# Where the first expert tiles' row gathers and index copies stand in the queues at the end of cross attention

## The chip, the core and the metric

One NeuronCore of a Trainium2 chip runs the whole kernel. The metric is the device time of one execution in microseconds (us); lower is better. The engines are TensorE (PE in the profile; its weight loads are PEld), VectorE (DVE), ScalarE (ACT), GpSimd (POOL) and SyncE (SP), which here only issues DMAs. Each engine works through its own queue in order, and they wait for one another on semaphores.

## The reference

A decoder block in fp32 on x of shape (4, 1024, 256), with post-norm after each of three parts:

```python
x = layernorm(x + gated_delta_attention(x))      # 4 heads, causal conv, recurrent state
x = layernorm(x + cross_attention(x, ctx, len))  # 16 heads of 64 over 77 context rows
x = layernorm(x + moe_ffn(x))                    # 8 experts, the best 2 of each token

# cross attention, for each token and head
scores = q @ k.T / 8 ; scores[:, col >= len] = -1e9
o = softmax(scores) @ v ; y = o @ Wo
# experts
probs = softmax(x @ router_w.T) ; keep the top 2, renormalised
h = silu(x @ gate_w[e] + gate_b[e]) * (x @ up_w[e] + up_b[e])
y = sum over the two e of probs[e] * (h @ down_w[e] + down_b[e])
```

## The kernel before, in words

The 4096 tokens are 32 tiles of 128 (`TILES`), in 8 blocks of 4 (`BLOCKS`, `BLK`). Four stages run one after the other: `project_stage`, `delta_stage`, `cross_stage`, `final_stage`. The experts are part of `cross_stage`: each engine's queue there is written out by hand, first its part of cross attention, tile by tile (`g` = 4n + t for tile t of block n), then its part of the experts' 71 tiles of 128 gathered rows (`FT`), numbered j.

Cross attention of tile g goes: scores in PSUM (TensorE, L1906), scaled out to `sc` (VectorE, L2278), mask added (GpSimd, `add_mask`, L1814), maximum taken and subtracted (VectorE, L2286, L2288), exponential (ScalarE, L2053), sum and reciprocal `den` (VectorE, `sums`, L2294, L2296), multiplied by `den` (GpSimd, `normed`, L1820). Then TensorE turns the weights (`weights_turned`, L1921, 10 transposes in three groups), ScalarE takes each group out of PSUM (L2062, L2065, L2067), and TensorE multiplies with the values (`attended`, L1930). The scores of tile g come two tiles ahead of its weights, so tile 31, the last, has no scores behind it to fill TensorE's queue. VectorE adds the residual for each pair of tiles (L2306).

While attention runs, the router works on blocks that are done: logits (TensorE, L1954), softmax and top two (VectorE, `shifted_logits`, `top_two`), positions of each row in its expert's list (`entries`, with the additions to `cum` at L2190), and the entries written to a `list` in HBM by indirect DMAs from GpSimd (`listed_rows`, L1805). In the last block, at t = 2 (tile 30), TensorE computes the logits of block 6 behind the attention of tile 30 and VectorE copies them out (`logits_out`, L2152). After five blocks the list holds enough full tiles for the first 32 expert tiles (`HEAD`), which can therefore start before the routing is complete.

An expert tile j needs: its 128 list rows (`expert_sync`, SP, L2461, to `rows`), their token numbers as integers (`expert_indices`, VectorE, L2611, to `idx`), an indirect gather of the tokens' rows of x2 from HBM (`expert_gather`, GpSimd, L2478), two transposes (TensorE, `x_turned`, L2522) taken out by ScalarE (L2581), gate and up products (L2533), the biases added by VectorE (L2624), SiLU by ScalarE (L2586), the product (VectorE, L2630), its transposes (L2543), the down product (L2554), bias and weight (L2637, L2639), and an indirect scatter with addition (GpSimd, L2492). Rows are loaded `LIST_LEAD` = 3 tiles ahead and gathered `ROW_LEAD` = 2 tiles ahead, so `rows` and `idx` of tiles 0, 1 and 2 and the gathers of 0 and 1 are issued during the last tiles of cross attention.

SP loads the down weights and bias (`load_experts_late`) and the gate and up biases (`load_experts_last`, L2419, two loads of 2 MB) in the last block. VectorE waits for them ahead of its first expert tile; the bias tile lies where attention's queries of odd blocks did.

The one wait of a gather that matters here, in `expert_gather`: `pool.wait_ge(x.idx_done, j + 1)`. `expert_indices` waits for `rows_in`.

Of the kernel before, what the change touches and what calls it, by code (L numbers as in the profile page):

```python
# [1631 lines left out]
def cross_stage(nc, a, s):  # L1632

    with ExitStack() as ctx:
# [77 lines left out]
        x = Experts(s, sem, x2_out, list_out, listed, at_done, row_bytes, row_idx,  # L1712
                    xs=[cut(of_kT, 0, D), cut(of_kT, D, D), cut(of_kT, 2 * D, D), cut(of_aT[1], 0, D)],
                    xsT=[cut(of_kT, 3 * D, D), cut(of_aT[1], D, D)],
                    g=[cut(sc[0], q * FF, FF) for q in R], u=[cut(sc[1], q * FF, FF) for q in R],
                    hT=[cut(of_aT[0], q * FK * P, FK * P) for q in R], o=[cut(of_vw, q * D, D) for q in range(4)],
                    pG=S[0:2], pU=[S[2], TB[0]], pX=TB[1], pH=Q, pD=O)
# [7 lines left out]
        TILE_N = BLOCKS * BLK  # L1725
# [56 lines left out]
        @block.gpsimd  # L1782
        def _(pool):
            nc.gpsimd.memset(powers[:], -0.5).then_inc(set_up, 1)
            nc.gpsimd.memset(eps[:, 1:2], XD * EPS).then_inc(set_up, 1)

            nc.gpsimd.memset(ent[:], 0.0).then_inc(set_up, 1)
            nc.gpsimd.memset(ids[:], 0.0).then_inc(set_up, 1)
            pool.wait_ge(set_up, 4)
            for t in T:  # L1790
                for k in R:
                    nc.gpsimd.tensor_scalar(ids[:, t, k, 1:2], con[:, C_COL:C_COL + 1],
                                            float(t * P), None, ALU.add).then_inc(set_up, 1)
                nc.gpsimd.tensor_scalar(ids[:, t, :, 2], con[:, C_COL:C_COL + 1].broadcast_to([P, 2]), float(t * P), None,
                                        ALU.add).then_inc(set_up, 1)
            for e in range(NE):
                nc.gpsimd.memset(cum[:, BLK, e:e + 1], float(e * REGION * P)).then_inc(set_up, 1)
            nc.gpsimd.tensor_scalar(k128[:], con[:, C_IOTA:C_IOTA + TILES], float(P), None, ALU.mult).then_inc(set_up, 1)

            def listed_rows(m, tiles):  # L1800

                pool.wait_ge(placed, m + 1)
                for t in tiles:
                    for k in R:
                        nc.gpsimd.indirect_dma_start(  # L1805
                            out=s["list"], out_offset=bass.IndirectOffsetOnAxis(ap=idx[:, k, t:t + 1], axis=0),
                            in_=ent[:, t, k, :], in_offset=None).then_inc(list_out, 16)

            def add_mask(g):
                b = g // BLK // 2  # L1810
                v = heads(sc[g % 2][:])
                pool.wait_ge(kv_in, 64 * b + 64)
                pool.wait_ge(sc_taken, 3 * g + 3)
                nc.gpsimd.tensor_tensor(v, v, madd[b % 2][:].unsqueeze(1).broadcast_to([P, XH, CTX]), ALU.add  # L1814
                                        ).then_inc(masked, 1)

            def normed(g):
                v = heads(sc[g % 2][:])
                pool.wait_ge(den_done, g + 1)
                nc.gpsimd.tensor_tensor(v, v, over_keys(den[g % 2][:]), ALU.mult).then_inc(scaled, 1)  # L1820

            def x2_deviations(n):
                pool.wait_ge(mv_done, n + 1)
                if n:
                    pool.wait_ge(x2_done, n)
                nc.gpsimd.tensor_scalar(rstd[:], mv[:, :, 1], EPS, None, ALU.add).then_inc(var_up, 1)
                pool.wait_ge(var_up, n + 1)
                nc.gpsimd.tensor_tensor(rstd[:], rstd[:], powers[:], ALU.pow).then_inc(r_done, 1)

            add_mask(0)  # L1830
            for n in range(BLOCKS):
                for t in T:
                    g = n * BLK + t
                    if g == TILE_N - 1:
                        for j in range(ROW_LEAD):
                            expert_gather(nc, pool, x, s, j)
                    normed(g)
                    if g + 1 < TILE_N:
                        add_mask(g + 1)
                    if n and t == 0:  # L1840
                        x2_deviations(n - 1)
                    if n >= 2 and t in (1, 2):
                        listed_rows(n - 2, (2 * t - 2, 2 * t - 1))

            def between(j):
                if j == 0:
                    x2_deviations(BLOCKS - 1)
                if 2 <= j < 2 + BLK:
                    listed_rows(BLOCKS - 2, (j - 2,))
                if 9 <= j < 9 + BLK:  # L1850
                    listed_rows(BLOCKS - 1, (j - 9,))

            expert_gpsimd(nc, pool, x, s, between)
            pool.wait_ge(list_out, 16 * BLOCKS * BLK * 2)
# [286 lines left out]
        def _(dve):  # L2141
# [115 lines left out]
            def rq_out(m):  # L2257
                dve.wait_ge(ssT_done, m + 1)
                if m:
                    dve.wait_ge(sc_taken, 3 * BLK * m)  # L2260
                sums = X[:].rearrange("p (t g i) -> p t g i", t=BLK, i=32)
                for k in range(2):
                    nc.vector.reciprocal(rq[:, :, 8 * k:8 * k + 8].rearrange("p t (g r) -> p t g r", r=2),
                                         sums[:, :, :, 2 * k:2 * k + 2]).then_inc((rq_half, rq_done)[k], 1)
# [65 lines left out]
            for n in range(BLOCKS):  # L2330
                for t in T:
                    g = n * BLK + t
                    if t == 2 and n + 1 < BLOCKS:
                        rq_out(n + 1)
                    if t == 2:
                        residual(n, 0)
                    if t == 0 and n:
                        residual(n - 1, 1)
                    if g + 1 < TILE_N:
                        maximum(g + 1)  # L2340
                        if t == 0 and n:
                            aggregated(n - 1)
                        sums(g + 1)
                    if t == 0 and n:
                        norm_terms(n - 1)
                    if g + 2 < TILE_N:
                        rider = None
                        if t == 2 and n:
                            rider = lambda frm, m=n - 1: logits_out(m, frm)
                        if t == 0 and n >= 2:  # L2350
                            rider = lambda frm, m=n - 2: counts_out(m, frm)
                        scaled_out(g + 2, rider)
                    if t == 2 and n == BLOCKS - 1:
                        dve.wait_ge(lg_done, 1)
                        logits_out(n - 1, X)
                    if t == 2 and n:
                        shifted_logits(n - 1)
                    if t == 3 and n:
                        top_two(n - 1)
                    if t == 0 and n >= 2:  # L2360
                        entries(n - 2)
                    if t and n == HEAD_BLOCKS + 1:
                        head_list(t - 1)
                    if g == TILE_N - 2:
                        for j in range(LIST_LEAD):
                            expert_indices(nc, dve, x, j)

            def between(j):
                if j == 0:
# [70 lines left out]
LIST_LEAD, ROW_LEAD = 3, 2  # L2440
# [24 lines left out]
def expert_gather(nc, pool, x, s, j):  # L2465

    q = j % 4
    if j == 0:
        pool.wait_ge(x.x2_out, 32 * HEAD_BLOCKS)
    if j == 3:  # L2470
        pool.wait_ge(x.at_done, BLOCKS * BLK)
    if j == HEAD:
        pool.wait_ge(x.x2_out, 32 * BLOCKS)
    pool.wait_ge(x.idx_done, j + 1)
    if j >= 4:
        pool.wait_ge(x.xT_done, j - 3)
    seen = HEAD_BLOCKS * BLK if j < HEAD else TILES
    nc.gpsimd.indirect_dma_start(  # L2478
        out=x.xs[q], out_offset=None, in_=s["x2"][0:seen].rearrange("t p d -> (t p) d"),
        in_offset=bass.IndirectOffsetOnAxis(ap=x.idx[j % 8][:, 1:2], axis=0)).then_inc(x.xs_in[q], 16)  # L2480
# [124 lines left out]
def expert_indices(nc, dve, x, j):  # L2605

    q = j % 8
    dve.wait_ge(x.rows_in[q], 16 * (j // 8) + 16)
    if j >= 8:
        dve.wait_ge(x.o_out[j % 4], 16 * (j // 4) - 16)  # L2610
    nc.vector.tensor_copy(x.idx[q][:], x.rows[q][:, 1:3]).then_inc(x.idx_done, 1)  # L2611
# [191 lines left out]
```

## Time and profile before

| | |
|---|---|
| median of 3 runs | 1705.97 us (1705.02 to 1707.05) |
| the profiled execution | 1707.56 us, its span 1705.8 us |
| mean granted TensorE clock | 0.951 |
| busy, share of the span | TensorE 89%, VectorE 64%, ScalarE 42%, GpSimd 39% |

Times in the trace count from the span's start. The change lies between 1190 and 1262 us; the expert tiles run from about 1237 to 1670, the final stage after that. A granted clock of 1.00 is TensorE's full speed (2.4 GHz), 0.50 half of it (1.2 GHz).

### The profile page before, as it was taken

The numbers are of one execution on the slowest core, as the hardware profiler recorded it, in microseconds if no ns is written. First come the engines' busy times: TensorE is split into PE (matmuls) and PEld (weight loads), VectorE is DVE, ScalarE is ACT, GpSimd is POOL, SyncE is SP. The second block draws the span as 40 slices with busy tenths as digits, with TensorE's granted clock in tenths as the row PEclk, the third lists the DMA queues.
The fourth block names the chain that finished last, engine by engine and source line by source line (L and its number), as shares of the span: only waits on it lengthen the run. The fifth ranks groups of instructions, "written<-read, shape, count | busy, mean of one in ns | idle before, by whom it ended". The sixth has DMA issues, their size and how long they took to land. (4 is left out here: it accounts for less than half of the span.)

```text
span 1705.8 us, 30447 instructions
## 1 busy us (share of the span) xinstructions
PE 1514.8 (89%) x10698; PEld 1075.5 (63%) x10698; DVE 1087.5 (64%) x2352; ACT 724.3 (42%) x1573; POOL 671.7 (39%) x526
## 2 busy tenths in 40 slices
PE   6999954799999999967999999997698999999990
PEld 3555523788888888643677777776555666666660
DVE  4899866577788875541458777888556444444543
ACT  4877751234444444454555455552242222222224
POOL 1354446212333311000434566654555544444440
PEclk9999976799999999989999999999799999999995
DMA  3233447645555535054034024110733332232226
GB/s 106 87 137 122 161 143 193 164 119 156 155 154 146 140 94 192 34 191 136 1 100 144 30 70 145 51 37 13 254 56 41 45 48 47 45 47 48 45 39 204
DMA packets 186795, 176.62 MB, mean 104 GB/s; under 512 B 79624, under 2 KB 147772, under 8 KB 186524
## 3 DMA queue, kind: packets, MB, share of 16 engines
q1 hardware_dynamic: 167659, 148.90, 28.8%
q0 software_dynamic: 17024, 22.43, 7.9%
q10 hardware_dynamic: 1968, 3.41, 0.7%
q8 instruction: 87, 1.43, 0.3%
q14 instruction: 57, 0.46, 0.1%
HBM read 110.67 MB, written 64.01 MB: 102 GB/s over the span
## 5 line engine op out<-in xcount | busy, mean ns | idle before, releaser
L2492 POOL DMA_INDIRECT y<-vw,idx x71 | 125.1, 1762 | 189.6 <-DVE vw L2639 178.3
L622 DVE SCALAR_TENSOR_TENSOR conv_y<-conv_in,taps,conv_y 128x512 f32<-128x512 f32 x192 | 161.4, 850 | 24.5 <-ACT conv_y L470 19.8
L2554 PE MATMUL xO<-late,aT 128*128 x568 | 134.5, 380 | 0.8 <-DVE vw L2637 0.8
L1876 PE MATMUL xQ<-late,last 128*128 128x512 f32 x256 | 124.8, 610 | 10.6 <-ACT late L2039 4.8
L2533 PE MATMUL xS<-w_gu,kT 128*128 x288 | 129.8, 593 | 0.4 <-issue 0.2
L375 PE MATMUL ps_j<-xnT,w_qkv 128*128 128x512 f32 x256 | 122.7, 603 | 0.0
L1820 POOL TENSOR_TENSOR sc<-sc,den 128x1232 f32<-128x1232 f32 x32 | 72.0, 2250 | 112.6 <-DVE den L2296 112.5
L2554 PEld LDWEIGHTS xO<-late,aT 128*128 128x128 f32 x568 | 102.4, 190 | 12.2 <-issue 1.2
L2624 DVE TENSOR_TENSOR sc<-xS,last 128x512 f32<-128x512 f32 x107 | 73.6, 691 | 54.3 <-PE xS L2533 50.6
L2637 DVE TENSOR_TENSOR vw<-xO,late 128x256 f32<-128x256 f32 x71 | 30.1, 424 | 119.5 <-PE xO L2554 110.0
L1814 POOL TENSOR_TENSOR sc<-sc,madd 128x1232 f32<-128x1232 f32 x32 | 82.7, 2585 | 32.7 <-DVE sc L2278 32.7
L2533 PEld LDWEIGHTS xS<-w_gu,kT 128*128 128x128 f32 x288 | 54.5, 190 | 54.1 <-issue 52.4
L1805 POOL DMA_INDIRECT list<-ent,idx x64 | 74.6, 1166 | 35.0 <-DVE ent L2204 18.2
L1000 POOL DMA_DIRECT2D x<-x1t x28 | 16.0, 572 | 183.4 <-ACT x1t L1352 183.4
L1930 PE MATMUL xO<-vw,aT 128*128 128x256 f32 (+1 forms) x320 | 78.8, 405 | 4.0 <-DVE x2t L2306 2.9
L1876 PEld LDWEIGHTS xQ<-late,last 128*128 128x128 f32 x256 | 45.2, 192 | 52.6 <-issue 31.2
L2294 DVE TENSOR_REDUCE den<-sc 128x16 f32<-128x1232 f32 x32 | 45.9, 1436 | 49.0 <-ACT sc L2053 49.0
L2581 ACT ACTIVATE kT<-xT 128x256 f32<-128x256 f32 x36 | 13.8, 382 | 146.8 <-PE xT L2522 142.5
L2581 ACT ACTIVATE aT<-xT 128x256 f32<-128x256 f32 x35 | 13.4, 383 | 146.2 <-PE xT L2522 141.8
L1930 PEld LDWEIGHTS xO<-vw,aT 128*128 128x128 f32 (+1 forms) x320 | 64.7, 205 | 16.7 <-issue 5.4
L1930 PE MATMUL xO<-last,aT 128*128 128x256 f32 (+1 forms) x320 | 72.0, 380 | 0.0
L1921 PE MATMUL xT<-con,sc 128*128 128x128 f32 x320 | 48.8, 287 | 25.8 <-POOL sc L1820 25.3
(359 smaller groups left out, 3664.2 us busy)
## 6 DMA issues: line engine op xcount, KB each, us to landing
carried<-qkvg SPq DMA_DIRECT2D x64, 256.0 KB, 4.0
qkvg<-tok SPq DMA_DIRECT2D x4, 2048.0 KB
qkvg<-gate SPq DMA_DIRECT2D x8, 1024.0 KB
qks<-qkvg SPq DMA_DIRECT2D x32, 256.0 KB, 4.6
steps<-step SPq DMA_DIRECT2D x30, 256.0 KB, 4.4
qkvg<-carried SPq DMA_DIRECT2D x3, 2048.0 KB
vw<-even SPq DMA_DIRECT2D x4, 1232.0 KB
xin<-in_x SPq DMA_DIRECT2D x9, 512.0 KB, 10.0
```

What stands on the lines that cost most here:

```text
L375: mm = pe.matmul(ps_j[j % 2][:], w_qkv[:, c, j * P:(j + 1) * P], xnT[b][:, c, :], start=c == 0, stop=c == KD - 1)
L622: y = nc.vector.scalar_tensor_tensor(conv_y[m % 4][:], conv_in[b][:, m, k:k + BT], taps[:, m, k:k + 1], conv_y[m % 4][:], ALU.mult, ALU.add)
L1805: nc.gpsimd.indirect_dma_start(out=s["list"], out_offset=bass.IndirectOffsetOnAxis(ap=idx[:, k, t:t + 1], axis=0), in_=ent[:, t, k, :], in ...
L1814: nc.gpsimd.tensor_tensor(v, v, madd[b % 2][:].unsqueeze(1).broadcast_to([P, XH, CTX]), ALU.add).then_inc(masked, 1)
L1820: nc.gpsimd.tensor_tensor(v, v, over_keys(den[g % 2][:]), ALU.mult).then_inc(scaled, 1)
L1876: mm = pe.matmul(Q[:], w_q[:, c, j * P:(j + 1) * P], x1T[:, c, :], start=c == 0, stop=c == KD - 1)
L1921: mm = pe.transpose(TB[u % 2][0:rows(c), i * P:(i + 1) * P], sc[g % 2][:, c * P:c * P + rows(c)], ident)
L1930: mm = pe.matmul(O[:, (g % 2) * D:(g % 2 + 1) * D], aT[g % 2][0:rows(c), c, :], vw[b % 2][0:rows(c), c, :], start=c == 0, stop=c == KCH - 1)
L2492: nc.gpsimd.indirect_dma_start(out=s["y"].rearrange("t p d -> (t p) d"), out_offset=bass.IndirectOffsetOnAxis(ap=x.idx[j % 8][:, 0:1], axi ...
L2533: mm = pe.matmul(to[:], x.xsT[q][:, c, :], w_gu[:, bass.ds(e, 1), c, k * FF:(k + 1) * FF], start=c == 0, stop=c == KD - 1)
L2554: mm = pe.matmul(x.pD[:, 0:D], x.hT[q][:, k, :], w_d[:, bass.ds(e, 1), k, :], start=k == 0, stop=k == FK - 1)
L2624: nc.vector.tensor_tensor(to, frm[:], b_gu[:, bass.ds(e, 1), k * FF:(k + 1) * FF], ALU.add).then_inc(done, 1)
```

## The change

On GpSimd the two gathers of expert tiles 0 and 1, which stood ahead of the normalisation of tile 31, now stand behind it. On VectorE the three index copies (expert tiles 0 to 2), which were the last thing in the turn of tile 30, behind the router's logits of block 6, are now issued ahead of the wait for those logits, directly behind the sums of tile 31. No instruction is added or removed.

```diff
@@ gpsimd queue of cross_stage
                 for t in T:
                     g = n * BLK + t
+                    normed(g)
+                    if g + 1 < TILE_N:
+                        add_mask(g + 1)
                     if g == TILE_N - 1:
                         for j in range(ROW_LEAD):
                             expert_gather(nc, pool, x, s, j)
-                    normed(g)
-                    if g + 1 < TILE_N:
-                        add_mask(g + 1)
                     if n and t == 0:
                         x2_deviations(n - 1)
@@ vector queue of cross_stage
                     if t == 2 and n == BLOCKS - 1:
+                        for j in range(LIST_LEAD):
+                            expert_indices(nc, dve, x, j)
                         dve.wait_ge(lg_done, 1)
                         logits_out(n - 1, X)
...
                     if t and n == HEAD_BLOCKS + 1:
                         head_list(t - 1)
-                    if g == TILE_N - 2:
-                        for j in range(LIST_LEAD):
-                            expert_indices(nc, dve, x, j)
```

## Rows read from the trace of the kernel before

**Rows 1.** The page, part 2: TensorE's granted clock in 40 equal slices, in tenths.

```profile
PEclk9999976799999999989999999999799999999995
```

**Rows 2.** Busy time of each engine (instructions), clock, DMA share and GB/s by stretch.

```profile
1200.00:1220.00 20.00, 14.24 (x57) 11.49 (x55) 12.21 (x17) 4.50 (x7) 13.89 (x10) 0.74 0.92 315
1220.00:1240.00 20.00, 13.13 (x52) 9.86 (x52) 6.42 (x28) 2.06 (x6) 5.09 (x5) 0.74 0.49 173
1300.00:1320.00 20.00, 15.60 (x61) 9.47 (x60) 9.60 (x20) 5.13 (x10) 13.28 (x12) 1.00 0.31 35
1620.00:1640.00 20.00, 20.00 (x80) 12.78 (x79) 9.50 (x20) 5.63 (x12) 10.01 (x8) 1.00 0.33 46
```

**Rows 3.** Timeline, 1190 to 1262: start, length, engine, line, what, [idle before, releaser].

```profile
1197.50 3.01 SPq L2461 DMA_DIRECT2D rows<-list  x3
...
1199.19 4.19 PEld L1930 LDWEIGHTS xO<-vw,aT 128*128 128x128 f32 x20
...
1210.07 3.08 SPq L2419 DMA_DIRECT2D last<-in_L_ffn_up_b  x1
...
1217.20 0.25 DVE L2296 RECIPROCAL den<-den 128x16 f32<-128x16 f32 x1
...
1219.17 1.85 PE L1954 MATMUL xX<-w_r,x2T 128*128 128x8 f32 x16
...
1221.61 0.30 DVE L2611 CAST idx<-rows 128x2 int32<-128x2 f32 x3
1222.57 0.99 POOL L2478 DMA_INDIRECT kT<-x,idx  x1 [6.04 <-DVE idx L2611]
...
1224.86 2.25 POOL L1820 TENSOR_TENSOR sc<-sc,den 128x1232 f32<-128x1232 f32 x1
...
1227.17 2.49 PE L1921 MATMUL xT<-con,sc 128*128 128x128 f32 x10 [6.15 <-POOL sc L1820]
...
1230.18 6.36 PEld L1930 LDWEIGHTS xO<-vw,aT 128*128 128x128 f32 x20 [0.96 <-ACT aT L2067]
...
1236.57 0.36 PEld L2522 LDWEIGHTS xT<-con,kT 128*128 128x128 f32 x2
...
1239.86 0.69 DVE L2624 TENSOR_TENSOR sc<-xS,last 128x512 f32<-128x512 f32 x1 [0.92 <-PE xS L2533]
...
1242.09 1.28 ACT L2586 ACT_TABLE_LOAD   x1
...
1245.85 0.47 PEld L2543 LDWEIGHTS xQ<-con,sc 128*128 128x128 f32 x4
```

**Rows 4.** TensorE in short stretches: length, busy (instructions), clock, DMA share, GB/s.

```profile
1192.50:1195.00 2.50, 0.01 (x1) 1.00 0.00 0
1207.50:1208.00 0.50, 0.00 (x0) 0.50 1.10 372
1224.50:1225.00 0.50, 0.00 (x0) 0.50 1.07 410
```

**Rows 5.** Timeline, 1176 to 1184: transposes and last eviction of tile 28.

```profile
1177.95 0.86 PEld L1921 LDWEIGHTS xT<-con,sc 128*128 128x128 f32 x8 [3.10 <-POOL sc L1820]
...
1179.95 0.26 ACT L2067 ACTIVATE aT<-xT 80x128 f32<-80x128 f32 x1
```

**Rows 6.** DMA view, 1209 to 1245 (median us to landing); tile `rows`, 1190 to 1262.

```profile
last<-in_L_ffn_up_b SPq DMA_DIRECT2D x1, 2048.0 KB, 20.5
...
DMA to landing us min/median/max: 6.4/7.4/8.4
```

**Rows 7.** GpSimd's DMA queue, 1219 to 1226, then 1226 to 1229.5: packets, MB, share.

```profile
q0 software_dynamic: 36, 0.00, 0.4%
...
q0 software_dynamic: 96, 0.26, 18.7%
```

**Rows 8.** By line, ns min/median/max: L2190 whole run; L1805 from 1195 to 1225.

```profile
L2190 DVE TENSOR_TENSOR cum<-cum,cnt x32: 166/167/2512, 926.8 to 1289.0; 128x8 f32<-128x8 f32 x32
...
L1805 POOL DMA_INDIRECT list<-ent,idx x8: 954/984/2150, 1200.6 to 1215.6; - x8
```

## The prediction

> **What bounds the kernel now.** I began with the page's slices of TensorE's granted clock: full or nearly so but for a few slices, of which the one with a 7 in the second half (number 28 counted from 0) is 1194 to 1237 us [rows 1]. The kernel is one long chain on TensorE, so a microsecond of TensorE idleness is a microsecond of time unless something behind it gives it back. The table by stage places the hole: of the 40 us from 1200 to 1240 TensorE is busy for 27.4, at a mean clock of 0.74; in the expert tiles as at 1620 to 1640 it is busy for all of a 20 us stretch at full clock, with one exception, 15.6 of 20 us at 1300 to 1320 [rows 2]. The expert tiles are thus a block that should slide with its start.
>
> The timeline from 1190 shows how tile 31, the last of cross attention, is reached [rows 3]. VectorE has the reciprocal `den` at 1217.45. All that `normed(31)` needs is there, and GpSimd has been idle since 1216.53 (1222.57 less its 6.04 of idle time). But the two gathers stand ahead of `normed(31)`, and they need index copies that VectorE issues behind the router's logits, which TensorE ends at 1221.02. So the chain is: logits 1221.02, index copies 1221.61, first gather 1222.57, second behind it, `normed(31)` 1224.86 to 1227.11, transposes 1227.17. TensorE idles for 6.15 us, and the row names GpSimd's `sc` as the releaser.
>
> **The change, part by part.** (1) Index copies. They go from 1221.61 to the end of `sums(31)`, 1217.45. They must have their rows. SP issued the three row loads from 1197.50; the last issue ended at 1200.51, and row loads land 6.4 to 8.4 us after issue where the trace shows it, so the last is in by about 1209 [rows 3, 6]. Bound: the copies of before ran at 1221.61 and show no wait. I take none. What is queued behind them on VectorE is `logits_out`, which cannot start before 1221.02, so 3.6 us cover three copies of 0.3 us in all. Nothing else is moved on VectorE.
>
> (2) `normed(31)`. GpSimd is free and starts 0.1 us behind `den`: 1217.53 to 1219.8, at the 2.25 us of its row. The multiply is then no longer what ends TensorE's wait. TensorE itself is: it runs attention of tile 30 and the logits until 1221.02. Transposes start at 1221.0 instead of 1227.17. **Gain 6.15 us.**
>
> The copies now run beside `normed(31)`, both on SBUF. The trace hints at what that can do: of 32 tiny `cum` additions on VectorE the median took 167 ns and the longest 2512, about the length of one GpSimd pass over the scores; of the eight GpSimd list writes from 1200.6 on the median issue took 984 ns, the longest 2150 [rows 8]. The Trainium skill (SBUF — State Buffer, "Who interferes with whom") says that the two engines share a port pair as an exclusive lock, so that whoever comes second blocks for a whole instruction; it speaks against this placement, and these two maxima agree with it. By that rule the last copies wait for the multiply's end at 1219.8. The price, from the rows: the copies end at 1220.1 at the latest, the multiply at 1220.1 if the copies hold it up instead, and a gather's issue grows by up to 1.2 us. Logits end at 1221.02, so the first two cost nothing; the third falls on the gathers' margin below.
>
> (3) The clock. The clock goes by what TensorE did before. The weight loads of tile 29's attention ended at 1203.38, and the granted clock stood at half at 1207.5; TensorE stopped at 1221.02, and it stood at half at 1224.5; idle time from 1192.5 to 1195 left it at full [rows 3, 4]. With the hole gone it is still at full when tile 31's transposes start, and the longest pause after that is the ScalarE evictions, about 1 us. So I expect full clock throughout. Tile 31 at half clock took 3.01 us from first transpose to attention's first weight load (1227.17 to 1230.18); tile 28 at full took 1177.95 to the end of its last eviction at 1180.21, 2.25, with 0.05 on top 2.3 [rows 5]. **Gain 0.7.** Attention's weight loads took 6.39 us from 1230.18 to the turn of the first expert tile at 1236.57; tile 29's at full clock 4.19. **Gain 2.2.** The first expert turn would start at about 1227.5 instead of 1236.57.
>
> (4) The gathers. GpSimd issues them after the multiply, at 1219.9 and 1221.2, 2.7 us earlier than before, but they must now be in by 1227.5, where before they had until 1236.57. They share the DMA engines with the bias loads. Before, gather 0 was issued at 1222.57; up to 1226 its queue moved only small packets of the list writes (36, 0.00 MB), and then, between 1226 and 1229.5, the 96 packets of both gathers (0.26 MB) [rows 7]. So gather 0 lands between 3.4 and 6.9 us after issue: 1223.3 to 1226.8. I take 1225.8, nearer the late end since the DMA engines are full, in time by 1.7 us. Gather 1 is needed only at the second turn, 4.7 us after the first. The Trainium skill (DMA: Bandwidth & Descriptors, "Queues, rings and completion order") says that each DMA engine alternates between the queues that have work, so a gather is not behind the whole bias load; the trace agrees in that the gathers moved while the bias load, landed at 1230.6, was still under way.
>
> (5) The bias loads themselves. `up_b` was issued at 1210.07 and lands 20.5 us later, at 1230.6 [rows 6]. VectorE waits for it ahead of its first expert addition, at 1239.86 before, at 1230.8 in the new order: just not a wait. If it is one, there is room. The first tile's gate half waits for ScalarE's table load (1242.09 to 1243.37), and TensorE takes the product's transpose only at 1245.85 [rows 3]: from the first addition at 1239.86 that is 6.0 us for two additions, the activation and the product, which by their own lengths need about 4 (an estimate). So the landing may slip by some 1.5 us past 1230.8 and TensorE feels nothing. What VectorE has ahead of that wait is on time as well: it had sat idle for 0.92 us before 1239.86, thus was done at 1238.9, and all of that hangs on tile 31's evictions and attention and moves with them, to 1229.9.
>
> Sum: 6.15 + 0.7 + 2.2 = 9.05 us. The profiled execution took 1707.56 us around a span of 1705.8, so its like would take 1698.5. It lies 1.6 above the median of 1705.97; against the median the forecast is **1696.9 us**.
>
> **The rivals.** A, as above: 1696.9, own range 1696.0 to 1698.2 (the margins under (4) and (5) touched lightly, and the runs' spread of 1 us).
>
> B, a transfer takes the place of the wait: gather 0 or the bias load is late. For it speaks that the margins are 1.7 and about 1.5 us and the DMA engines are busy for 0.92 of 1200 to 1220 [rows 2]. At the worst gather 0 is in when the shared drain of before ended, 1229.5: the turn 2.0 us late, gain 7.0, 1698.9. Time 1697.8 to 1699.
>
> C, the clock falls anyway in tile 31 because of the pauses between its pieces: only the 6.15 us remain, 1699.8. Against it: full clock survived a longer pause at 1192.5 [rows 4].
>
> D, the gain is given back among the expert tiles, so that the time is within 0.2% of before. The place would be 1301 to 1318, where TensorE waits 4.4 of 20 us for gathers that stand behind GpSimd's scatters and list writes. Two such stretches more are 8.8 us and give 1705.7. Against it: these waits are between instructions that all slide together, and no load with a fixed date lies behind 1231.
>
> E, slower: the copies hold VectorE because the third tile's rows come late. What VectorE has to do from there to the first expert addition is its 6.42 us of work at 1220 to 1240 [rows 2]. That ends later than 1239.86 only if the rows come after 1233.4, and the kernel is 0.2% slower from 1236.8; the copies at 1221.61 exclude that for the execution traced. For an arrival at 1237.5 the time would be 4.1 above the median, 1710.1.
>
> The change not doing what it says: it would need TensorE to wait at 1221 for something else than `scaled`; but the row of 1227.17 names `sc` of GpSimd as what came last, so I give it nothing of its own.
>
> **How the numbers follow.** A 0.60, B 0.20, C 0.10, D 0.07, E 0.03. 0.2% is 3.4 us, about what a measurement of this kernel can tell from no change. A, B and C are all faster by more: 0.90, to which I add 0.02 of D that gives back only half; same 0.05, slower 0.03. The range takes in A, B and C with the runs' spread on both ends: 1695.3 to 1700.5.
>
> **What would show it.** Right: GpSimd's multiply L1820 for tile 31 starts 0.1 us after `den`, ahead of the gathers; TensorE's idle time before the last L1921 group is gone, the group takes less than 2.49 us, the clock is 1.0 from 1218 on; the first L2522 stands near 1227.5; everything from there to the end is 9 us earlier. Wrong: L2522 or the first L2624 waiting on a DMA (B), a half clock in attention 31 (C), more TensorE idle time than 5 us after the first 60 us of the expert tiles (D), copies L2611 long after `den` (E).

## The result

| | before | changed |
|---|---|---|
| median of 20 runs | 1706.96 us | 1698.7 us |
| lowest to highest | 1702.9 to 1714.33 | 1693.95 to 1706.1 |
| profiled execution, span | 1705.8 us | 1700.0 us |

The ratio is 0.9951 with a 95% interval of 0.9939 to 0.9963: 8.4 us faster, 6.3 to 10.4 at the interval's ends. The forecast was 9.05 us and 1696.9, from a median of 1705.97 over the first three runs; from the 1706.96 of all twenty it would be 1697.9. The ratios in this text leave out two runs at a granted clock of 0.55 and 0.64, one of e1_gathers_only (2663.37 us) and one of the kernel before beside e1 to e4 (2320.02 us).

The timeline of the changed kernel at the end of cross attention follows. Its columns are those of [rows 3], whose rows it answers to; from `expert` on, a line number is one lower than before (the gather is L2477, the first turn L2521, the bias addition L2623, the product's transposes L2542).

```profile
1213.67 2.70 SPq L2418 DMA_DIRECT2D last<-in_L_ffn_up_b  x1
...
1219.99 0.25 DVE L2296 RECIPROCAL den<-den 128x16 f32<-128x16 f32 x1
1220.16 0.24 DVE L2610 CAST idx<-rows 128x2 int32<-128x2 f32 x3
1220.33 2.24 POOL L1820 TENSOR_TENSOR sc<-sc,den 128x1232 f32<-128x1232 f32 x1 [1.01 <-DVE idx L2610]
...
1221.23 1.85 PE L1954 MATMUL xX<-w_r,x2T 128*128 128x8 f32 x16
1222.73 1.02 POOL L2477 DMA_INDIRECT kT<-x,idx  x1 [0.16 <-issue]
...
1222.94 1.07 PE L1921 MATMUL xT<-con,sc 128*128 128x128 f32 x8
...
1225.22 4.18 PEld L1930 LDWEIGHTS xO<-vw,aT 128*128 128x128 f32 x20 [0.79 <-ACT aT L2067]
...
1229.43 0.36 PEld L2521 LDWEIGHTS xT<-con,kT 128*128 128x128 f32 x2
...
1235.20 1.29 DVE L2623 TENSOR_TENSOR sc<-xS,last 128x512 f32<-128x512 f32 x2 [3.40 <-PE xS L2532]
...
1236.90 0.69 DVE L2629 TENSOR_TENSOR sc<-sc 128x512 f32<-128x512 f32 x1 [0.41 <-ACT sc L2585]
...
1238.71 0.47 PEld L2542 LDWEIGHTS xQ<-con,sc 128*128 128x128 f32 x4
```

In this execution the last `den` ends at 1220.24, 2.79 us later than before, although nothing ahead of it differs; everything is therefore read against that moment. The copies follow it at 1220.16 and the multiply at 1220.33, at once. The multiply is over at 1222.57, and TensorE, which runs the logits until 1223.08, goes on into the transposes (1222.94) without a wait. No gather is waited for. The first turn (the two transposes with which an expert tile begins on TensorE) has its weight load at 1229.43.

| from `den` = 0, us | before | changed |
|---|---|---|
| index copies | 4.16 | -0.08 |
| multiply starts | 7.41 | 0.09 |
| first gather starts | 5.12 | 2.49 |
| transposes of tile 31 (first matmul) | 9.72 | 2.70 |
| attention 31 (first weight load) | 12.73 | 4.98 |
| first expert turn (weight load) | 19.12 | 9.19 |

The turn comes 9.93 us earlier. Of this the span shows 5.8: 2.79 had gone into the later `den`, the block of expert tiles took 1.1 longer and what follows it 0.3. Part of the 9.93 is no work of the change: the logits end 3.57 us after `den` in the execution before and 2.84 in this one. Counted from the logits' end the turn's first matmul comes at 15.77 before and at 6.57 here, 9.2 us earlier. Three of the stretches that answer to [rows 2]:

```profile
1200.00:1220.00 20.00, 15.85 (x67) 13.08 (x66) 14.40 (x30) 5.38 (x10) 14.28 (x11) 0.77 0.88 279
1220.00:1240.00 20.00, 17.98 (x84) 12.26 (x83) 10.11 (x36) 6.55 (x14) 7.55 (x7) 1.00 0.69 244
1300.00:1320.00 20.00, 16.91 (x60) 10.51 (x59) 7.31 (x14) 4.28 (x9) 13.90 (x12) 0.91 0.38 42
```

TensorE is busy for 17.98 of 20 us from 1220 on at full clock, where it was 13.13 at 0.74. In the stretch from 1300 the clock is 0.91, where it was 1.00: here this execution's block loses its 1.1 us. Columns as in [rows 4]:

```profile
1304.50:1305.00 0.50, 0.50 (x6) 0.69 0.11 8
...
1308.00:1308.50 0.50, 0.50 (x3) 0.90 0.54 49
```

TensorE waits in both kernels at that place; here the clock went to half just as the work went on. It is no cost of the change that these runs show: in its second execution, e7 below, the block took 412.83 us, 0.4 less than before the change.

### The profile page after: what moved, and what is told of

It reads as the page before. It is cut to its first block and busy times, and to the rows that moved or that the text cites. A ratio compares the mean times of both kernels' runs of the same rounds, so it can differ in the third digit from the quotient of the medians.

```text
span 1700.0 us, 30447 instructions
## 1 busy us (share of the span) xinstructions
PE 1518.7 (89%) x10698; PEld 1077.3 (63%) x10698; DVE 1086.1 (64%) x2352; ACT 725.2 (43%) x1573; POOL 673.1 (40%) x526
## 5 line engine op out<-in xcount | busy, mean ns | idle before, releaser
L1876 PE MATMUL xQ<-late,last 128*128 128x512 f32 x256 | 128.5, 626 | 10.6 <-ACT late L2039 4.8
L2623 DVE TENSOR_TENSOR sc<-xS,last 128x512 f32<-128x512 f32 x107 | 73.5, 691 | 55.7 <-PE xS L2532 51.1
L1805 POOL DMA_INDIRECT list<-ent,idx x64 | 74.6, 1166 | 35.0 <-DVE ent L2204 18.1
L375 PEld LDWEIGHTS ps_j<-xnT,w_qkv 128*128 128x128 f32 x256 | 46.3, 195 | 41.3 <-issue 41.3
```

The lines of the kernel that those rows point to most:

```text
L375: mm = pe.matmul(ps_j[j % 2][:], w_qkv[:, c, j * P:(j + 1) * P], xnT[b][:, c, :], start=c == 0, stop=c == KD - 1)
L1805: nc.gpsimd.indirect_dma_start(out=s["list"], out_offset=bass.IndirectOffsetOnAxis(ap=idx[:, k, t:t + 1], axis=0), in_=ent[:, t, k, :], in ...
L1876: mm = pe.matmul(Q[:], w_q[:, c, j * P:(j + 1) * P], x1T[:, c, :], start=c == 0, stop=c == KD - 1)
L2623: nc.vector.tensor_tensor(to, frm[:], b_gu[:, bass.ds(e, 1), k * FF:(k + 1) * FF], ALU.add).then_inc(done, 1)
```

## The experiments

Each line of this table is one profiled execution. "Turn" is the time from the end of the last `den` to the start of the first turn's matmul (19.34 before, 9.41 in the changed kernel; the weight load is 0.2 earlier). "Block" is the time from there to the start of the 71st turn. The ratio is to the kernel before on the same chip. Between executions `den` itself lies anywhere from 1210.0 to 1221.45 us, so spans are compared only through these two pieces, and times only through the ratios. A third piece, from the start of the 71st turn to the end of the span, is 55.5 to 56.1 us in eight of the ten, and 58.8 and 58.9 in e5 and e6.

| kernel | `den` ends | turn | block | ratio (95%) |
|---|---|---|---|---|
| before | 1217.45 | 19.34 | 413.24 | 1 |
| changed | 1220.24 | 9.41 | 414.38 | 0.9951 (0.9939 to 0.9963) |
| e1_gathers_only | 1216.04 | 10.48 | 414.60 | 0.9962 (0.9945 to 0.9980) |
| e2_copies_only | 1210.00 | 15.11 | 412.16 | 0.9978 (0.9961 to 0.9995) |
| e3_fill_hole | 1221.45 | 15.77 | 413.98 | 0.9995 (0.9978 to 1.0012) |
| e4_late_bias | 1219.23 | 10.03 | 420.51 | 0.9995 (0.9977 to 1.0013) |
| e8_copies_only_fill | 1213.11 | 12.16 | 412.76 | 0.9961 (0.9940 to 0.9982) |
| e5_spread_lists | 1215.25 | 9.48 | 409.68 | 0.9939 (0.9921 to 0.9957) |
| e6_spread_fill | 1217.91 | 9.12 | 409.46 | 0.9937 (0.9913 to 0.9961) |
| e7_changed_again | 1214.05 | 10.03 | 412.83 | 0.9954 (0.9937 to 0.9971) |

**e1_gathers_only.** Of the diff only the GpSimd half.

```diff
@@ gpsimd queue, against before
+                    normed(g)
+                    if g + 1 < TILE_N:
+                        add_mask(g + 1)
                     if g == TILE_N - 1:
                         for j in range(ROW_LEAD):
                             expert_gather(nc, pool, x, s, j)
-                    normed(g)
-                    if g + 1 < TILE_N:
-                        add_mask(g + 1)
```

> The kernel before with only the GpSimd half of the change: the gathers of expert tiles 0 and 1 behind the last normalisation; the index copies stay behind the logits. My theory (TensorE waits only for the normalisation; the gathers have room): the first expert turn comes 9.4 to 11 us after the last reciprocal of the denominators, against 19.3 before and 9.4 after the change, because the first gather now starts about 2 us later than in the changed kernel and lands just in time or up to 2 us late; the time is 0.4 to 0.55% below that of before. Rival (the index copies are what matters): the turn waits for the gather by 5 us or more and the gain is under 0.25%.

Its timeline:

```profile
1216.13 2.24 POOL L1820 TENSOR_TENSOR sc<-sc,den 128x1232 f32<-128x1232 f32 x1 [1.00 <-DVE den L2296]
...
1220.99 1.01 POOL L2478 DMA_INDIRECT kT<-x,idx  x1 [2.62 <-DVE idx L2611]
...
1221.58 4.18 PEld L1930 LDWEIGHTS xO<-vw,aT 128*128 128x128 f32 x20 [0.79 <-ACT aT L2067]
...
1226.52 0.41 PE L2522 MATMUL xT<-con,kT 128*128 128x128 f32 x2 [0.36 <-DMA kT<-x,idx]
```

The multiply starts 0.1 us after `den`. The gather must wait for copies that still stand behind the logits and is issued at 1220.99, 4.95 us after `den` against 2.49 in the changed kernel. Now TensorE does wait for it, 0.36 us, until 1226.52: the gather was under way for 5.5 us from the start of its issue. The turn at 10.48 lies in the expected 9.4 to 11. Its logits end 3.39 us after `den`, so from their end the turn comes at 7.09, against 15.77 before and 6.57 in the changed kernel: the GpSimd half alone brings 8.7 of the 9.2 us, and the index copies are worth about 0.5 us, by which they keep the gather off the path. The ratio, 0.38%, is below the expected 0.4 to 0.55 by its centre, with an interval that holds all of it.

**e2_copies_only.** Of the diff only the VectorE half.

```diff
@@ vector queue, against before
                     if t == 2 and n == BLOCKS - 1:
+                        for j in range(LIST_LEAD):
+                            expert_indices(nc, dve, x, j)
                         dve.wait_ge(lg_done, 1)
...
-                    if g == TILE_N - 2:
-                        for j in range(LIST_LEAD):
-                            expert_indices(nc, dve, x, j)
```

> The kernel before with only the VectorE half: the index copies ahead of the logits, the two gathers still ahead of the last normalisation. My theory: the gathers run 2.6 us from the reciprocal on, the normalisation ends 4.9 us after it, TensorE idles about 1.4 us behind the logits instead of 6.2, the clock stays at full, and the first expert turn comes 10.8 us after the reciprocal: a gain of 8.5 us or 0.5%. Rival (each half is worth its share of the 6.15 us hole and the clock falls all the same): the turn comes at about 15, a gain of 0.25%.

Its timeline, and below it TensorE in short stretches (length, busy, clock, DMA share, GB/s):

```profile
1210.83 0.99 POOL L2477 DMA_INDIRECT kT<-x,idx  x1 [1.75 <-DVE idx L2610]
...
1213.12 2.25 POOL L1820 TENSOR_TENSOR sc<-sc,den 128x1232 f32<-128x1232 f32 x1
...
1213.92 1.51 DVE L2158 TENSOR_TENSOR pr<-lg,row 128x32 f32<-128x32 f32 x1
...
1215.43 1.09 PE L1921 MATMUL xT<-con,sc 128*128 128x128 f32 x8 [2.00 <-POOL sc L1820]
...
1217.98 6.89 PEld L1930 LDWEIGHTS xO<-vw,aT 128*128 128x128 f32 x20 [0.97 <-ACT aT L2067]
```

```profile
1213.50:1215.50 2.00, 0.07 (x1) 1.00 0.96 276
...
1216.50:1217.00 0.50, 0.25 (x2) 0.67 0.90 352
1217.00:1217.50 0.50, 0.46 (x2) 0.50 1.57 393
```

The hole behind the logits is 2.00 us, as expected to within 0.6. But the clock falls at 1216.5 to 1217, and attention of tile 31 takes 6.9 us of weight loads, as it did before the change. The turn is at 15.1, where I had 10.8, and the rival's number, 15, is met for the reason it gave. My ground for full clock had been a pause of 2.5 us that left it at full [rows 4]; a pause of 2.0 us here did not. The row of 1213.92 is a by-result: VectorE's subtraction of two SBUF tiles took 1.51 us beside the multiply and ended with it, against 0.19 in the changed kernel.

**e8_copies_only_fill.** The same, with TensorE kept at work in that pause.

```diff
@@ tensor queue, against e2_copies_only
                     if t == 2 and n == BLOCKS - 1:
                         logits(n - 1, X).then_inc(lg_done, 1)
+                        pe.wait_ge(q_sb, BLOCKS * XJ)
+                        for _ in range(2):
+                            pe.matmul(Q[:], con[:, 0:P], con[:, 0:512], start=True, stop=True)
```

> The copies-only kernel with two idle matmuls (into the free query bank, result unused) behind the logits, in the 2.0 us for which TensorE waited there for the last normalisation. In the copies-only execution the granted clock fell to half 3 us after that pause began, under tile 31's transposes, and attention of tile 31 took 6.9 us. My theory (that fall, and nothing else, cost the copies-only kernel its second 4 us): the pause is filled, the clock stays at full, and the first expert turn comes 10.9 us after the last reciprocal instead of 15.1. Rival (something in the order of gathers and normalisation slowed tile 31): the turn stays near 15.

```profile
1213.93 0.99 POOL L2480 DMA_INDIRECT kT<-x,idx  x1 [1.74 <-DVE idx L2613]
...
1216.36 1.96 PE L2017 MATMUL xQ<-con 128*128 128x512 f32 x4
...
1218.53 1.09 PE L1921 MATMUL xT<-con,sc 128*128 128x128 f32 x8 [0.21 <-POOL sc L1820]
...
1220.84 4.18 PEld L1930 LDWEIGHTS xO<-vw,aT 128*128 128x128 f32 x20 [0.79 <-ACT aT L2070]
...
1225.05 0.36 PEld L2524 LDWEIGHTS xT<-con,kT 128*128 128x128 f32 x2
```

With the pause filled the clock stays at full and attention's weight loads take 4.2 us again (1220.84 to 1225.05). The turn falls from 15.1 to 12.2, so the fall of the clock was what the copies-only kernel lost. Expected was 10.9. Of the 1.3 us too many, 0.7 are my own addition (4.9 to the multiply's end, 2.3, 4.2 and the 0.2 of the weight load make 11.6), and 0.5 are that the multiply ends 5.4 us after `den` and not 4.9: GpSimd starts the first gather 0.66 us after the copies end. The order with the gathers first is still 2.1 to 2.8 us behind the two executions of the changed kernel: that is what the GpSimd half is worth with the clock taken out.

**e3_fill_hole.** The queues of before, with idle matmuls in the hole.

```diff
@@ tensor queue, against before
                     if t == 2 and n == BLOCKS - 1:
                         logits(n - 1, X).then_inc(lg_done, 1)
+                        pe.wait_ge(sc_taken, 3 * TILE_N)
+                        for _ in range(6):
+                            pe.matmul(S[0][:], con[:, 0:P], con[:, 0:512], start=True, stop=True)
```

> The kernel before with six idle matmuls (128 by 512, fp32, into a free PSUM bank, their result unused) behind the logits, in the 6.15 us for which TensorE waits for the last normalisation. The order of the queues is that of before. My theory (the change won 6.15 us of waiting and 2.9 us of clock): the wait stays, the granted clock stays at full through tile 31's transposes and attention, the first turn comes 16.4 us after the reciprocal instead of 19.3, and the kernel gains 2.9 us, 0.17%. Rival (the whole gain is waiting, and the clock term was put together wrongly from two tiles): the turn stays at 19 and the time within 0.05% of before.

```profile
1224.19 5.40 PE L2017 MATMUL xS<-con 128*128 128x512 f32 x12
...
1230.49 1.09 PE L1921 MATMUL xT<-con,sc 128*128 128x128 f32 x8 [0.90 <-POOL sc L1820]
...
1232.80 4.18 PEld L1930 LDWEIGHTS xO<-vw,aT 128*128 128x128 f32 x20 [0.79 <-ACT aT L2070]
...
1237.01 0.36 PEld L2525 LDWEIGHTS xT<-con,kT 128*128 128x128 f32 x2
```

Transposes to turn take 6.52 us (1230.49 to 1237.01) against 9.40 before [rows 3] and 6.49 in the changed kernel. That is the clock term alone, 2.88 us, where the prediction had 0.7 + 2.2 = 2.9. The turn at 15.77 is 0.6 below the expected 16.4 because the transposes themselves came 9.04 us after `den`, not 9.72, the logits having ended 2.88 us after it and not 3.57. The measured ratio, 0.9995 with 0.17% to either side, cannot tell 0.17% from nothing; the trace can.

**e4_late_bias.** The changed kernel with the biases made late.

```diff
@@ sync queue, against changed
+                    sp.dma_start(s["spare"], a["L0_ffn_down_w"][0:4]).then_inc(spare_in, 16)
                     load_experts_last(sp, a, s)
...
+        "spare": dram("spare", [4, FF, D]),
```

> The changed kernel with a copy of 2 MB inside HBM issued ahead of the two bias loads, so that the biases land 5 to 10 us later; the copied data is not used. In the changed kernel the first bias addition waited until 1235.20, 2.5 us past where the rest had it ready, and TensorE lost nothing. My theory (there is about 1 us of room left and then the landing sets the start of the expert tiles): TensorE stands still in front of the transposes of the first product for the delay less 1 us, and the time is 4 to 9 us above that of the changed kernel, near that of before. Rival (the biases are not on the path, or the loads share the bandwidth so that they hardly move): the time is that of the changed kernel, 0.5% below before.

```profile
1229.26 0.41 PE L2524 MATMUL xT<-con,kT 128*128 128x128 f32 x2 [0.49 <-DMA kT<-x,idx]
...
1240.35 1.29 DVE L2626 TENSOR_TENSOR sc<-xS,last 128x512 f32<-128x512 f32 x2 [9.58 <-issue]
...
1242.49 1.11 PE L2545 MATMUL xQ<-con,sc 128*128 128x128 f32 x4 [3.64 <-DVE sc L2632]
...
1245.65 5.33 PE L2535 MATMUL xS<-w_gu,kT 128*128 x8
```

The first bias addition starts at 1240.35, 21.1 us after `den` against 15.0 in the changed kernel. Now TensorE stands for 3.64 us before the transposes of the first product, and what follows runs at half clock for a while: eight matmuls take 5.33 us (3.69 in the changed kernel). The third gap between turns grows from 5.69 to 12.35 us, 6.7 us in one place. The time returns to that of before. How late the biases may be before it costs anything can be read from this. From the turn to the transposes of the product (weight loads) it was 9.28 us before and 9.28 in the changed kernel, in spite of a bias addition 2.5 us late; the product was ready at 1237.59, 1.1 us before TensorE took it. Here the addition comes another 5.4 us later against the turn and the transposes 4.0, so that 1.4 us were left in the changed kernel and the whole room was 3.9. From the first addition to the transposes the chain itself takes 2.1 us (1240.35 to 1242.49). The first gather also landed later, 7.5 us after its issue, and held the turn up by 0.5 us.

**e5_spread_lists.** What the block of expert tiles gives back. The two list writes of each of four expert tiles become one for each of eight.

```diff
@@ gpsimd queue, against changed
-                if 9 <= j < 9 + BLK:
-                    listed_rows(BLOCKS - 1, (j - 9,))
+                if 10 <= j < 10 + 2 * BLK:
+                    listed_rows(BLOCKS - 1, ((j - 10) // 2,), ((j - 10) % 2,))
```

> The changed kernel with the eight list writes of the last block spread: one for each expert tile from 10 on instead of two for each from 9 on. It bears on what the block of expert tiles gives back: in the changed kernel the turns of tiles 12, 13 and 14 come 10.1, 7.6 and 6.5 us after the one before, against 5.8 in a tile without extra work, 6.7 us in all, 1.1 more than before the change, with the clock at half for part of it. My theory (GpSimd's two list writes for each tile put the gather behind what TensorE can use, and the pause then takes the clock down): the three come within 1 us of 5.8 each, last turn to first turn is 409 to 411 us instead of 414.4, and the kernel is 3 to 5 us faster than the changed one, 0.7 to 0.8% below before. Rival (VectorE's list of the remaining tiles, 5 us long, is what delays tile 11 and all behind it): the gap stays at 9 us or more and the time is that of the changed kernel.

First the changed kernel at that place, GpSimd and then TensorE, each a timeline of one engine:

```profile
1297.46 0.98 POOL L1805 DMA_INDIRECT list<-ent,idx  x1 [0.30 <-issue]
1298.74 0.96 POOL L1805 DMA_INDIRECT list<-ent,idx  x1 [0.30 <-issue]
1300.00 1.01 POOL L2477 DMA_INDIRECT kT<-x,idx  x1 [0.30 <-issue]
```

```profile
1304.18 0.44 PE L2521 MATMUL xT<-con,kT 128*128 128x128 f32 x2 [2.62 <-DMA kT<-x,idx]
...
1305.08 3.39 PE L2553 MATMUL xO<-late,aT 128*128 x8
```

Two list writes stand ahead of the gather of 1300.00; TensorE waits 2.62 us for it, the clock has fallen, and the first down product takes 3.39 us instead of 1.89. The spread kernel, TensorE:

```profile
1291.34 0.66 PE L2542 MATMUL xQ<-con,sc 128*128 128x128 f32 x4 [1.30 <-DVE sc L2629]
...
1296.99 0.38 PE L2521 MATMUL xT<-con,kT 128*128 128x128 f32 x2
```

The turns of tiles 12, 13 and 14 follow the one before at 7.33, 5.82 and 5.82 us: two of the three delays are gone (10.1, 7.6 and 6.5 us in the first execution of the changed kernel; 9.4, 6.0 and 6.5 in e7). The 1.5 us that stay are the rival's: the product waits 1.30 us for VectorE, which makes the list of the remaining tiles there. The block takes 409.7 us against 414.4 and 412.8 in two executions of the changed kernel, inside the expected 409 to 411. But the time was expected 0.7 to 0.8% below before, 3 to 5 us under the changed kernel, and is 0.61% below; the medians are 1697.1 and 1697.9 for the control beside it, the ratios 0.9939 and 0.9954 with intervals that overlap. Most of what the block gained is lost behind it. GpSimd's first instruction of the final stage with its idle time before it, in this kernel and then in the control e7:

```profile
1664.12 0.10 POOL L2690 MEMSET eps<- 128x1 f32 x1 [9.59 <-POOLq L100]
```

```profile
1663.84 0.10 POOL L2690 MEMSET eps<- 128x1 f32 x1 [6.09 <-POOLq L100]
```

From the issue of the last scatter to the start of the final stage it takes 11.1 us here and in e6, and 7.4 to 7.7 in the other eight executions; in the queue of GpSimd the trace has a DRAIN at the end of the stage (L1634) of 5.77 us here and 2.30 in e7. With the last scatter 0.7 us sooner after the last turn, 2.7 us of the 3.2 by which the block is shorter than the control's are gone again. Why the wait at the stage's end is longer when the list writes are spread, no run here shows.

**e6_spread_fill.** The spread kernel with TensorE's two pauses filled.

```diff
@@ tensor queue, against e5_spread_lists
                     if t == 2 and n == BLOCKS - 1:
                         logits(n - 1, X).then_inc(lg_done, 1)
+                        for _ in range(2):
+                            pe.matmul(Q[:], con[:, 0:P], con[:, 0:512], start=True, stop=True)
+                    if t == 1 and n == BLOCKS - 1:
+                        pe.wait_ge(q_sb, BLOCKS * XJ)
+                        for _ in range(5):
+                            pe.matmul(Q[:], con[:, 0:P], con[:, 0:512], start=True, stop=True)
```

> The spread kernel with idle matmuls in two pauses of TensorE at the end of cross attention: five between attention of tile 29 and the transposes of tile 30, two behind the logits (into the free query bank, result unused). My theory (tile 30 at half clock now sets when the logits end, and behind it the last reciprocal is the next bound): attention of tile 30 takes 4.5 us instead of 7, the logits end 2 to 3 us earlier, the transposes of tile 31 wait for the normalisation, 2.4 us after the reciprocal, and the first expert turn comes 8.3 to 8.9 us after the reciprocal instead of 9.4; of that up to 1 us goes to the wait for the biases. At most 0.07% under the spread kernel. Rival (the biases are the bound already): the first product's transposes stay where they are and the time is that of the spread kernel.

```profile
1216.19 1.85 PE L1954 MATMUL xX<-w_r,x2T 128*128 128x8 f32 x16
1217.66 0.25 DVE L2302 RECIPROCAL den<-den 128x16 f32<-128x16 f32 x1
...
1220.30 1.09 PE L1921 MATMUL xT<-con,sc 128*128 128x128 f32 x8 [0.44 <-POOL sc L1820]
...
1222.60 4.18 PEld L1930 LDWEIGHTS xO<-vw,aT 128*128 128x128 f32 x20 [0.79 <-ACT aT L2073]
...
1226.81 0.36 PEld L2527 LDWEIGHTS xT<-con,kT 128*128 128x128 f32 x2
```

The logits now end at 1218.04, 0.1 us after `den`, where they ended at 2.84 in the changed kernel, and the transposes wait for the multiply: 2.39 us after `den`. The next bound is the chain of the denominators, as expected, but it lay only 0.3 us below the old one. Attention of tile 30 runs at full clock, 4.6 us instead of 7.0. The turn at 9.12 misses the expected 8.3 to 8.9 and is 0.3 below the lower of the two executions of the changed kernel (9.41 and 10.03). The transposes of the first product follow it by 9.28 us as before, so the biases were not the bound. Filling these pauses is worth nothing that these six runs can tell on top of the spread lists. Both versions lie below the changed kernel by their medians, 1697.1 and 1696.1 (six runs) against the control's 1697.9; none of it is clear of the intervals.

**e7_changed_again.** The control.

> The changed kernel unaltered, as the control of this group on the same chip. My theory (the shift of the first expert turn against the last reciprocal is set by the queues, the rest by where the clock happens to fall): the turn comes 9.4 us after the reciprocal again, within 0.5 us unless a clock fall reaches tile 31, and the ratio to before is 0.994 to 0.9965. Rival (the 9.9 us were one execution's luck): the turn lies 2 us or more away from 9.4.

The turn came at 10.03, 0.12 us outside the half microsecond I allowed. The logits' first matmul started 1.62 us after `den` here and 0.99 there: it is the end of attention 30 that moves it. There the transposes of tile 30 ran partly at full clock (2.04 us, here 2.49), attention began 0.45 us earlier against `den` and took 7.04 us, here 7.20. From the logits' end the turn comes at 6.56, there at 6.57. The 9.9 us are no luck of one execution; a spread of 0.6 us belongs to them, and 9.2 us is what both show once the logits' end is taken as the mark.

The bias loads in this execution, two lines of the timeline and one of the DMA view (median us to landing):

```profile
1207.04 3.02 SPq L2418 DMA_DIRECT2D last<-in_L_ffn_up_b  x1
...
1228.52 1.29 DVE L2623 TENSOR_TENSOR sc<-xS,last 128x512 f32<-128x512 f32 x2 [2.28 <-issue]
```

```profile
last<-in_L_ffn_up_b SPq DMA_DIRECT2D x1, 2048.0 KB, 20.4
```

The biases land 20.4 us after issue, at 1227.4, and the addition that needs them starts 1.1 us later. In e4 it is the same: landing 26.6 us after the issue at 1212.72, addition at 1240.35, 1.05 later. Between the wait for the biases and the addition the kernel reads the number of the tile's expert into a register (`expert`, L2443); in the trace that read starts at the landing.

## Why the prediction was right

(1) Index copies. Right: no wait, 0.24 us for three, right behind `den`. E1 prices them at about 0.5 us.

(2) The multiply, forecast at 0.1 us after `den`: 0.09. The transposes were forecast at the logits' end: so they came. The term was 6.15 us and measured 7.0 against `den` (9.72 to 2.70), because in the changed execution the logits ended 2.84 us after `den` instead of 3.57, and the transposes overlap them by 0.1. That is the spread at the end of attention 30 seen in e7, not the change, and so 0.7 us of the 9.9 are luck. The clash over the port pair did not arise: the copies were done 0.07 us after the multiply began, which took 2.24 us. Where an operation does stand beside it, in e2, VectorE's subtraction of two SBUF tiles ended with the multiply, 1.51 us for an instruction of 0.19. The Trainium skill (SBUF — State Buffer, "Who interferes with whom") says that a VectorE instruction with two SBUF inputs contends with a GpSimd instruction that reads SBUF, and that the one issued second blocks; the trace agrees.

(3) The clock. The size was right twice, 2.88 us in e3 by itself and 2.91 in the changed kernel (9.40 less 6.49), where the forecast was 0.7 + 2.2 = 2.9. The argument for it was weaker than it looked. It held where the change leaves no pause of the matmuls longer than 0.53 us at that place; "full clock survived a longer pause" is refuted by e2, where 2.0 us of pause were followed by half clock. The Trainium skill (TensorE: Matmul & The Clock Gate, "Part 1: The HAM clock gate") says that the monitor runs free of the kernel, so that the point at which the clock changes varies from run to run. A 2.5 us pause without a fall [rows 4] and a 2.0 us pause with one fit that, though the work around the two pauses differs as well, so that these rows do not show it by themselves. In an order of queues that leaves 2 us of pause, rival C's fall is what happened.

(4) The gathers. Issued at 2.49 us after `den` (forecast 2.45), in time. The landing was put at 3.4 to 6.9 us, 5.9 taken. E1, where TensorE waits for one, measures 5.5; e4, with 2 MB more under way, 7.5. The landing is on record for the first gather of e8, 6.2 us after its issue. With 5.5 to 6.2 us the margin in the changed kernel was 0.5 to 1.2 us (an estimate), not 1.7.

(5) The biases. This step was off. I had the wait of VectorE at "just not"; it was 2.5 us (due 3.3 us after the turn, as before, at 1232.7; started at 1235.20). The landing itself was right, 20.4 us after issue in e7 for the 20.5 taken. What I had wrong is what follows it: the read of the expert's number stands behind the wait, so the addition starts 1.1 us after the landing, and I had read the 0.92 us of idle time ahead of the addition before the change as spare time. The rest is that the issue came 0.8 us later against `den` in that execution, and the turn 0.9 us earlier than forecast. The room for it was underrated as well, which saved the forecast: I had 1.5 us, from a chain of about 4 us from the first addition to the transposes, and e4 measures 2.1 for the chain, so that TensorE lost nothing at 2.5 us, with 1.4 left. E4 bears out that a landing later still is paid in full and then takes the clock with it.

(6) The block of expert tiles slid as a whole: it was 1.1 us longer than before in one execution of the changed kernel and 0.4 shorter in the other. Rival D named the place where the block varies, and no loss there can be laid to the change. Rivals B and E did not occur; E's premise, late rows, is seen in no execution.

The sum was 9.05; the two executions of the changed kernel show 9.9 and 9.3 up to the turn (19.34 less 9.41 and less 10.03), and the medians 8.4 in all, with 6.3 to 10.4 for the interval. From the logits' end both show 9.2.

## What to carry to other kernels

When an engine's queue holds work that the critical chain needs behind work that is merely early, look first for what the early work waits for: here a 2.25 us multiply stood ready while two prefetches ahead of it waited on a third engine. A hole on TensorE costs its length and, if the clock falls, the work after it at half speed as well; a filler in the hole of the old order measures that second part by itself. Before closing a hole, list the transfers whose landing the later start had hidden, and price each against the new start: the next two here, a gather and a bias load, had about 0.5 to 1.2 and 1.4 us left. And follow a gain to the end of the kernel: of the 3.2 us that spreading the list writes took off the expert tiles, 2.7 came back at the end of the stage.

## What the runs showed that I had not expected

The same instructions reach the last `den` at 1210.0 to 1221.5 us in ten executions, a spread of 11 us, larger than the change. Nearly all of it was there by the first tile of cross attention: the first multiply by `den` started between 802.4 and 813.8 us, and from there to the last `den` it is 407.6 to 407.9 us in all ten. So single executions of this kernel say nothing about 8 us in their span, and a great deal if read from a common mark.

GpSimd starts an indirect DMA 0.66 us after the copy it waited for has ended (e2, e8, e1 and the kernel before), but 0.16 us after its own multiply.

A gather of 128 rows of 1 KB, 131 KB in all, took 5.5 us from issue to use beside the bias loads (e1) and 7.5 us with another 2 MB in flight (e4).
